# Attention pass of a decoder layer: the cap of exp(K+U) on GpSimd, behind the low part of the last chunk's y; VectorE mixes R ahead of weighing V

## What is computed

```
R = mixed_r(x) @ Wr.T + br;  K = mixed_k(x) @ Wk.T + bk;  V = mixed_v(x) @ Wv.T + bv
e  = exp(clip(W + K, -20, 10))             # W: -relu(decay) * steps that remain
eu = exp(clip(U + K, -20, 10))
A = shift(cumsum(e * V)) + eu * V
B = shift(cumsum(e)) + eu
out = (sigmoid(R) * A / B) @ Wo.T + bo
```

## Time and profile before

| | |
|---|---|
| runs, median (lowest to highest) | 1376.91 us (1374.55 to 1377.23) |
| the profiled execution | 1377.34 us |
| its span in the trace | 1375.3 us |
| TensorE, share of the span | 1327.4 us, 97% |
| VectorE | 1090.5 us, 79% |
| ScalarE | 813.5 us, 59% |
| GpSimd | 634.0 us, 46% |
| the attention pass | from 0 to about 760 us |

### The profile page before, as it was taken

The page is one execution under the profiler, slowest core; times in us unless marked ns, Lnnn a source line. Parts: engine busy times, 40 slices in busy tenths (PEclk is TensorE's granted clock), DMA queues, the critical chain, the costliest instruction groups (busy, mean ns, idle before and its releaser), DMA issues. The chain is left out here.

```text
span 1375.3 us, 19352 instructions
## 1 busy us (share of the span) xinstructions
PE 1327.4 (97%) x6330; PEld 1098.3 (80%) x6330; DVE 1090.5 (79%) x1782; ACT 813.5 (59%) x1555; POOL 634.0 (46%) x558
## 2 busy tenths in 40 slices
PE   5899999999999999999999999999999899999998
PEld 4777887887888878878886778888888778888886
DVE  6999989889899898898988776655555677777774
ACT  5875666656666666666665464444446366666664
POOL 4665344343443433434434544444445455555552
PEclk9999999999999999999999999999999999999999
DMA  9010101001001010010050354444443312222212
GB/s 349 9 30 2 61 31 50 13 31 61 13 17 61 31 58 3 31 61 0 1 222 1 138 210 168 150 146 153 166 147 120 104 59 92 91 91 91 92 62 92
DMA packets 54539, 113.92 MB, mean 83 GB/s; under 512 B 2768, under 2 KB 7120, under 8 KB 52560
## 3 DMA queue, kind: packets, MB, share of 16 engines
q1 hardware_dynamic: 54480, 113.22, 23.2%
HBM read 88.05 MB, written 25.17 MB: 82 GB/s over the span
## 5 line engine op out<-in xcount | busy, mean ns | idle before, releaser
L818 POOL TENSOR_TENSOR a_ss<-a_ss,a_eu 128x512 f32<-128x512 f32 x64 | 82.7, 1293 | 281.4 <-DVE a_ss L630 281.4
L612 DVE SCALAR_TENSOR_TENSOR bank<-bank,k_or_row 128x510 f32<-128x510 f32 x192 | 132.8, 692 | 56.3 <-ACT k_or_row L494 53.3
L823 POOL TENSOR_TENSOR a_sv<-a_sv,a_euv 128x512 f32<-128x512 f32 x64 | 82.8, 1294 | 119.0 <-DVE a_sv L647 119.0
L494 ACT ACTIVATE k_or_row<-bank 128x512 f32<-128x512 f32 x192 | 113.8, 593 | 5.7 <-PE bank L82 0.5
L514 ACT ACTIVATE bank<-bank,a_nbr 128x510 f32<-128x510 f32 x64 | 42.3, 661 | 123.0 <-DVE bank L612 123.0
L401 PE MATMUL bank<-a_wo_hi,a_y_hi 128*128 128x512 f32 x256 | 100.4, 392 | 0.0
L401 PE MATMUL bank<-a_wo_hi,a_y_lo 128*128 128x512 f32 x256 | 99.7, 389 | 0.0
L401 PE MATMUL bank<-a_wo_lo,a_y_hi 128*128 128x512 f32 x256 | 99.6, 389 | 0.0
L1510 POOL TENSOR_TENSOR b_cx_lo<-b_cx,b_cx_hi 128x512 fp32r<-128x512 f32 x32 | 40.6, 1299 | 113.2 <-ACT b_cx_hi L1205 113.2
L827 POOL TENSOR_TENSOR a_y_lo<-a_yy,a_y_hi 128x512 fp32r<-128x512 f32 x64 | 85.6, 1337 | 3.6 <-ACT a_y_hi L537 3.6
L526 ACT ACTIVATE bank<-a_ss 128x512 f32<-128x512 f32 x64 | 38.7, 604 | 74.8 <-DVE a_ss L653 74.8
(11 more groups left out here) (246 smaller groups left out, 4719.4 us busy)
## 6 DMA issues: line engine op xcount, KB each, us to landing
xres<-in_x SPq DMA_DIRECT2D x8, 1024.0 KB, 5.3
x_after_attention<-xres SPq DMA_DIRECT2D x8, 1024.0 KB, 4.3
xin<-x_after_attention SPq DMA_DIRECT2D x8, 1024.0 KB, 5.6
b_ct<-in_ctx_t SPq DMA_DIRECT2D x8, 1024.0 KB, 6.5
b_cx<-in_ctx SPq DMA_DIRECT2D x8, 1024.0 KB, 7.7
xres<-x_after_attention SPq DMA_DIRECT2D x8, 1024.0 KB, 5.7
x_after_cross<-xres SPq DMA_DIRECT2D x8, 1024.0 KB, 4.4
xin<-x_after_cross SPq DMA_DIRECT2D x8, 1024.0 KB, 5.5
```

What stands on the lines that cost most here:

```text
L494: sc.activation(u3[:, :, 1:], ps[m][:, :, :], ACT.Copy, scale=MIX[m]).then_inc(left[m], 1)
L612: ve.scalar_tensor_tensor(out=ps[m][:, :, 0:T - 1], in0=ps[m][:, :, 1:T], scalar=1.0 - MIX[m], in1=u3[:, :, 0:T - 1], op0=ALU.mult, op1=AL ...
L818: gp.tensor_tensor(ss3[:, :, 0:T], ss3[:, :, 0:T], eu[:, :, :], ALU.add).then_inc(b_done, 1)
L823: gp.tensor_tensor(sv3[:, :, 0:T], sv3[:, :, 0:T], euv[:, :, :], ALU.add).then_inc(a_done, 1)
```

## The change

The cap of eu leaves VectorE's `clip` and becomes `clip_own` on GpSimd, with the same bounds. `weigh_own` now waits for it. On VectorE `mix("r")` goes ahead of `weigh_own`. On GpSimd `y_rest(g - 1)` goes from behind `above(g)` to the front of the chunk, behind a wait for `eu_exp`; `clip_own(g)` follows it, then `below(g)` and `above(g)`.

```diff
@@ -621,7 +621,6 @@
                                         op0=ALU.mult, op1=ALU.add).then_inc(arg_done, 1)
 
             def clip(g):
-                ve.tensor_scalar(eu[:, :, :], eu[:, :, :], CLIP_LO, CLIP_HI, ALU.max, ALU.min).then_inc(eu_clip, 1)
                 dve.wait_ge(e_exp, g + 1)
                 ve.tensor_scalar(ee3[:, :, 1:], ee3[:, :, 1:], CLIP_LO, CLIP_HI, ALU.max, ALU.min).then_inc(e_clip, 1)
 
@@ -632,6 +631,7 @@
             def weigh_own(g, c):
 
                 dve.wait_ge(edge_v, g + 1)
+                dve.wait_ge(eu_clip, g + 1)
                 wait(dve, a_done, g)
                 ve.scalar_tensor_tensor(out=euv[:, :, :], in0=ps["v"][:, :, :], scalar=col[:, 2, c:c + 1],
                                         in1=eu[:, :, :], op0=ALU.add, op1=ALU.mult).then_inc(euv_done, 1)
@@ -744,8 +744,8 @@
                     mix("v", g)
                     clip(g)
                     scan_e(g)
+                    mix("r", g)
                     weigh_own(g, c)
-                    mix("r", g)
                     weigh(g, c)
                     scan_ev(g)
                     if 3 <= c < 3 + KC and ahead:
@@ -812,6 +812,11 @@
                 gp.tensor_tensor(piece(n)[2], raw(n), piece(n)[1].bitcast(F32),
                                  ALU.subtract).then_inc(wlo_done["kvro"[n % 4]], 1)
 
+            def clip_own(g):
+                if isinstance(g, int) and g == 0:
+                    pool.wait_ge(eu_exp, 1)
+                gp.tensor_scalar(eu[:, :, :], eu[:, :, :], CLIP_LO, CLIP_HI, ALU.max, ALU.min).then_inc(eu_clip, 1)
+
             def below(g):
                 pool.wait_ge(eu_clip, g + 1)
                 pool.wait_ge(s_scan, g + 1)
@@ -849,10 +854,12 @@
                     g = i * HC + c
                     if c == 1 and not is_last(i):
                         rstd_of(i + 1)
+                    if c > 0 or not is_first(i):
+                        pool.wait_ge(eu_exp, g + 1)
+                        y_rest(g - 1, (c - 1) % HC)
+                    clip_own(g)
                     below(g)
                     above(g)
-                    if c > 0 or not is_first(i):
-                        y_rest(g - 1, (c - 1) % HC)
                     if is_first(i) and c < HC - AHEAD:
                         for m in range(1, 4):
                             split_rest(4 * (c + AHEAD) + m)
```

## The result

The changed kernel takes **1489.30 us**, the median of 4 runs (1487.22 to 1489.89), against 1376.73 (1374.55 to 1377.23, 4 runs) for the kernel before on the same chip: ratio 1.082, 95% interval 1.081 to 1.083. The prediction was 1414, with a range of 1403 to 1447. So the sign is right and the size is not: 112 us are lost where 37 were forecast.

What follows compares the result with a forecast made beforehand. A loop through VectorE and ScalarE was taken as the bound, 90.81 us per tile. Middle tiles +30.6, first tile +2 and last +4 gave +36.6 on 1377.34, so 1414 us, range 1403 to 1447.

Steps and rivals of the forecast that it cites:

- What bounds the kernel: Attention pass: a loop through VectorE and ScalarE sets the pace, 90.81 us per tile; a longer VectorE list lengthens it.
- rival 3: Idle 1.19 us ahead of the mix of K is slack and absorbs the delay; time stays at 1377; chance 0.04.
- The scan is held by `y_rest`: VectorE's `scan_e` waits for GpSimd's `y_rest` at the front of the chunk, ends at 2.67 and loses 1.1 us.
- Rival 1: `scan_e` is not held by `y_rest`; 1361 us, or about 1385 with a dear cap; chance 0.13.
- The steps up to the cap: In a chunk, from the cap of e: `y_rest` ends at 1.58, `scan_e` at 2.67, mix of R starts at 2.59.
- The price of the cap: `clip_own` on GpSimd, called c: taken as 0.76 us, between bounds 0.42 and 1.29, making `weigh` 0.80 us later.
- The four chances: Chances given to the outcomes: forecast 0.60, rival 2 0.23, rival 1 0.13, rival 3 0.04.
- The 0.20 us saved in chunks with `xt_rest`: VectorE's `xt_rest` already waits 0.20 us for ScalarE's input, so these chunks lose 0.60 instead of 0.80.
- Rival 2: Slower still: `scan_e` goes ahead of `y_rest` (1431 us), or the cap costs as much as an add (1445); chance 0.23.
- The scan goes first: `scan_e` wins over `y_rest`, which ends at 2.85; `weigh` comes 1.08 us later; 1431 us.
- A dear cap: `clip_own` on GpSimd costs 1.29 us, as an add does; `weigh` is at 4.50; 1445 us.

Runs made afterwards that it cites:

- Experiment 3: The changed kernel with the mix of R put back behind `weigh_own` on VectorE: 1533.29 us, ratio 1.114.
- Experiment 4: Changed kernel with GpSimd's cap of eu first, `y_rest` back behind `above`: 1370.01 us; with the first tile's cap on VectorE as well: 1364.96 us.
- the first of the two cap-first versions: Changed kernel with the cap of eu first on GpSimd in all tiles and `y_rest` back behind `above`: 1370.01 us, ratio 0.995.

## Why the prediction was right in sign and wrong in size

**What bounds the kernel: right.** VectorE's list between the mix of V and the denominator is a part of a loop. The 1.19 idle ahead of the mix of K stayed in every version with a longer list, so rival 3 is out: the delay was never absorbed.

**The scan is held by `y_rest`: right, and seen for the first time here.** 1.23 became 2.23 in all chunks but two of the first tile, and the kernel with that order alone lost 54 us. Rival 1, the scan that is not held, is out. (The prediction's own steps, 0.46 to 2.67, give 2.21 for the scan; its "near 2.3" and "loses 1.1" were loose.) The Trainium skill (SBUF — State Buffer, Who interferes with whom) made no exception for a scan with two SBUF inputs, and this measured 1.23 to 2.23 agrees with it.

**The steps up to the cap: right.** Forecast and measured, from the cap of e: `y_rest` ends at 1.58 and at 1.61, the scan ends at 2.67 and at 2.70, the mix of R starts at 2.59 and at 2.62. The forecast had `y_rest` wait for the cap of e; here it took its clear 1.29, so this trace doesn't show that wait. `weigh` without any cap: 3.83 and 3.85.

**The price of the cap: this is the step that failed.** "Its price c has no row", said the prediction; it took 0.76, "half of that for one input", between bounds of 0.42 and 1.29. Measured: 1.92. With 1.92 in place of 0.76 and nothing else changed, `weigh` is 1.96 later instead of 0.80. A middle tile is 90.81 + 4 x 1.96 + 4 x 1.76 = 105.7 (measured 106.3), six of them 86.3 more than before (89.1). The first tile loses 8 x 1.96 - 3.8 = 11.9 (9.4), the last 8 x (12.56 - 10.91) = 13.2 (13.4). The sum is 1377.3 + 111.4 = 1489, the measured time. That it meets it to the microsecond is luck: the middle tiles are 2.8 short and the first tile is 2.5 over. But the steps were nearly enough; one number in them was far off.

The reasoning that gave c has two faults. It took the cost per element from an instruction with another operation, as if the number of inputs alone decided; the rows with `mult` and `add` show that this is nearly right for arithmetic (0.61) and three times too low for `max` and `min`. And the upper bound, a two-input add, was the dearest row at hand, not a bound: nothing in the trace said that a single-input instruction can't be slower than an add. The four chances added up to 1, all inside 1361 to 1445, so none was left for a price above that bound. The Trainium skill (GPSIMD Engine Reference, 4.1 Engine selection) has one-input operations at roughly line rate. The 0.61 us of the arithmetic form, against VectorE's 0.42, comes near to that; the 1.92 of the cap does not.

**The 0.20 us saved in chunks with `xt_rest`: right.** They went from 11.43 to 13.19, by 1.76, and plain ones from 10.60 to 12.60, by 2.00; the difference is 0.24. It is there only with the mix of R ahead (Experiment 3).

**Rival 2** had both its halves as alternatives. "The scan goes first" occurs in one chunk, where `y_rest` comes a little later (chunk 2 above); in all others that have a `y_rest` it was first. "A dear cap" is what came true, and further than its 1445, since the cap is dearer than the add that it was priced by.

**What is not settled:** why `max` and `min` are slow on GpSimd. Only these two together, `min` alone, and `mult` with `add` were run, all on 32-bit floats and with constants of their own. How much of the gain in Experiment 4 is the cap's and how much the mix of R's is not settled either.

## What to carry to other kernels

Moving an instruction to an idle engine saves its old duration and costs its new one, at the place where the result is needed; if that engine has no row of the same operation in the trace, take no other operation's slope as a bound, but say that the price is open upward, or measure it first. The same move gained or lost by where it stood: 1.92 us in front of the waiting instruction cost 85 us, or 6%; with the same 1.92 us in GpSimd's idle time, 3.4 us earlier in most chunks, the kernel came out 0.5 to 0.8% faster than before, with the mix of R's share in it. And an instruction with two SBUF inputs on GpSimd should not be put where VectorE runs one of its own: that alone cost 3.9% here.

## What the runs showed of the hardware beyond this

The prediction had it that one engine waits for the whole of the other's instruction. For GpSimd's add and VectorE's scan this holds. For the slow cap on GpSimd it holds one way only. When the scan is under way, the cap waits for it (2.71 instead of 1.92). But a scan that starts late in the cap is not held, and does not lengthen it: in the first of the two cap-first versions this stands in chunk 1 (GpSimd, then VectorE).

```profile
39.03 1.93 POOL L818 TENSOR_SCALAR a_eu<-a_eu 128x512 f32<-128x512 f32 x1
```

```profile
39.69 0.42 DVE L625 TENSOR_SCALAR a_ee<-a_ee 128x512 f32<-128x512 f32 x1
40.15 1.23 DVE L629 TENSOR_TENSOR_SCAN a_ss<-a_mask,a_ee 128x514 f32<-128x514 f32 x1
```

The scan starts 0.81 us before the cap's end and takes its 1.23. A scan that starts near the cap's beginning does lose something, but not the whole cap. Chunk 0 of the changed kernel, GpSimd and then VectorE:

```profile
24.51 1.99 POOL L818 TENSOR_SCALAR a_eu<-a_eu 128x512 f32<-128x512 f32 x1
```

```profile
24.75 1.51 DVE L629 TENSOR_TENSOR_SCAN a_ss<-a_mask,a_ee 128x514 f32<-128x514 f32 x1
```

Held for the whole cap, the scan would have ended behind 26.50 by more than a microsecond; it ended at 26.26, 0.28 us late. VectorE's cap of e is undisturbed when it starts 1.14 us or more before the end of GpSimd's cap, as in chunk 1 above. When it starts 0.22 to 0.51 before that end, as in 50 chunks of that version (chunk 34 in Experiment 4), it always ends 0.27 to 0.29 behind it (0.51 to 0.78 us instead of 0.42). So the slow instruction is in VectorE's way for a part of its time only, and not in the way of every kind of instruction alike. Why is open; no run was made on it.
